# Scale and bias of the latents and of the first tile as columns behind their transposes, and a new order of the first transfers

## What is computed

```python
def layernorm(x, g, b, eps=1e-05):
    m = jnp.mean(x, axis=-1, keepdims=True)
    v = jnp.mean((x - m) ** 2, axis=-1, keepdims=True)
    return (x - m) / jnp.sqrt(v + eps) * g + b
...
xn = layernorm(x, ln_x_g, ln_x_b)
ln = layernorm(latents, ln_l_g, ln_l_b)
q = (ln @ Wq).reshape(b, m, h, d).transpose(0, 2, 1, 3)
kv = jnp.concatenate([xn @ Wkv, ln @ Wkv], axis=1)
...
qn = rmsnorm(q, qn_g) * scale
kn = rmsnorm(k, kn_g)
sim = jnp.einsum('bhid,bhjd->bhij', qn, kn)
```

## Time and profile before

| what | value |
|---|---|
| median of 3 runs | 240.18 us (240.14 to 240.39) |
| the profiled execution | 239.64 us |
| its span | 237.8 us |
| busy: PE, DVE, ACT, POOL | 225.6, 153.7, 150.0, 80.8 us |
| mean granted clock of TensorE | 0.993 |

### The profile page before, as it was taken

One profiled execution on the slowest core, in us unless ns is written; L12 is line 12 of the kernel. 1 busy time (PEld: TensorE's weight loads), 2 busy tenths in 40 slices (PEclk: granted clock), 3 DMA queues, 4 the chain that ended last, 5 costly groups with the idle time before them and its releaser, 6 DMA issues.

```text
span 237.8 us, 4203 instructions
## 1 busy us (share of the span) xinstructions
PE 225.6 (95%) x1475; PEld 194.6 (82%) x1475; DVE 153.7 (65%) x346; ACT 150.0 (63%) x329; POOL 80.8 (34%) x127
## 2 busy tenths in 40 slices
PE   7688999999989999999999999999999998999994
PEld 7354887786778989888898879899999987999883
DVE  1779999998688876867668655566665540312541
ACT  3355589889876769695766567777777655015141
POOL 5468776772464637473250500000000010100200
PEclk9799999999999999999999999999999999999999
DMA  5875101010000000000000799600000000000000
GB/s 181 301 216 206 48 22 44 25 31 16 1 21 3 0 6 0 0 0 3 0 3 0 240 428 328 160 0 3 0 4 0 0 4 0 0 3 0 0 3 22
DMA packets 11236, 13.80 MB, mean 58 GB/s; under 512 B 1584, under 2 KB 9936, under 8 KB 10960
## 3 DMA queue, kind: packets, MB, share of 16 engines
...
...
## 4 chain that ended last, share of the span: by engine, by line
PE 68%; DVE 15%; ACT 5%; POOL 4%; issue 4%; DMA 3%; SPq 1%; ACTq 0%; DVEq 0%; POOLq 0%
PE banks L1135 17%; PE banks L1010 13%; PE banks L1057 8%; PE banks L1086 8%; DVE small L778 5%; PE banks L1264 5%; PE banks L1156 4%; DVE sk L790 3%; DMA rows<-in_L_xattn_ln_x_b 3%; PE banks L1149 3%; PE banks L1088 2%; PE banks L1187 2%; PE banks L1289 1%; DVE raw L746 1%; POOL small L459 1%
## 5 line engine op out<-in xcount | busy, mean ns | idle before, releaser
L813 DVE TENSOR_TENSOR ptl<-banks,pth 128x512 fp32r<-128x512 f32 (+1 forms) x48 | 26.8, 558 | 28.6 <-ACT pth L576 27.6
L1135 PE MATMUL banks<-xnh,pth 128*128 128x256 f32 x128 | 37.6, 294 | 0.0
L1135 PE MATMUL banks<-xnh,ptl 128*128 128x256 f32 x128 | 36.3, 284 | 0.0
L1135 PE MATMUL banks<-xnl,pth 128*128 128x256 f32 x128 | 36.2, 283 | 0.0
L576 ACT ACTIVATE pth<-banks 128x512 fp32r<-128x512 f32 (+1 forms) x48 | 23.7, 493 | 11.3 <-PE banks L1010 10.2
L459 POOL TENSOR_TENSOR small<-small 128x16 f32<-128x16 f32 x7 | 20.4, 2908 | 29.2 <-DVE small L785 29.2
L523 ACT ACTIVATE sk<-banks 128x512 f32<-128x512 f32 x36 | 20.5, 606 | 13.4 <-PE banks L1057 13.3
L790 DVE TENSOR_TENSOR sk<-banks,small 128x512 f32<-128x512 f32 x36 | 23.0, 679 | 7.0 <-POOL small L459 6.9
L778 DVE TENSOR_REDUCE small<-sk 128x8 f32<-128x512 f32 x36 | 23.5, 678 | 4.0 <-ACT sk L523 3.9
L440 POOL COPY sp<-sp 128x64 f32<-128x64 f32 x16 | 4.1, 255 | 63.0 <-ACT sp L557 63.0
L1010 PE MATMUL banks<-ident,sp 128*128 128x128 f32 x144 | 24.4, 280 | 1.1 <-ACT sp L557 1.0
...
## 6 DMA issues: line engine op xcount, KB each, us to landing
knT<-in_L_attn_qkv_kernel SPq DMA_DIRECT2D x1, 3072.0 KB, 12.0
raw<-in_ctx SPq DMA_DIRECT2D x16, 128.0 KB, 2.1
knT<-in_L_xattn_Wq SPq DMA_DIRECT2D x1, 1024.0 KB, 9.2
wv<-in_L_xattn_Wkv SPq DMA_DIRECT2D x1, 1024.0 KB, 5.3
wout_sb<-in_L_xattn_Wout SPq DMA_DIRECT2D x1, 1024.0 KB, 5.5
knT<-in_L_attn_out_kernel SPq DMA_DIRECT2D x1, 1024.0 KB, 14.6
...
```

The lines of the kernel that those rows point to most:

```text
L813: nc.vector.tensor_tensor(ptl[:, j0:j1, :], banks[:, t3_bank(u, c), 0:(j1 - j0) * P].rearrange("p (j r) -> p j r", j=j1 - j0), pth[:, j0:j ...
L1135: nc.tensor.matmul(banks[:, u_bank(u), 0:D], p_[:, j, :], x_, start=(j == 0 and i == 0), stop=False)
```

## The change

In words, by engine:

- *Queues.* The four vectors ln_l_g, ln_l_b, ln_x_g and ln_x_b are also read as they lie, 2 rows of 128 each, into gb8 (8 x 128): two from SP's queue behind x, two from ScalarE's queue behind its weights. The rows of ln_l move behind tile 3 and the query weights, the rows of ln_x from behind tile 0 to behind tile 1, the query weights from behind tile 1 to behind tile 2. The latents' copies and the value weights move from behind tile 4 to behind tile 7. Tile 4 also waits for tile 0's transposes.
- *TensorE.* A transpose turns gb8 into 8 columns. The transposes of the latents and of tile 0 read the centred, scaled rows, without gain and bias. Item 0's second half takes its third product before the second. Keep_clock's 10 become 9 ahead of the latents and 4 behind.
- *ScalarE.* It copies the columns to gcols. For the latents and tile 0 it then applies gain and bias, which are now one number a partition, as it copies from the bank (scaled): twice each, once for xth and once in full fp32 (lnTf, x0Tf). L636's copy moves from item 3 to item 7.
- *VectorE.* The latents are centred and scaled in one operation in place of two. The low halves of the latents and of tile 0 are taken from the full copies. Statistics and centring of tiles 1 to 4 and sums of tile 5 stand at other places.
- *GpSimd.* The latents' rows lnf are made here, in item 1 (two operations of 128x256). The gains' product moves from item 0 to item 2, and tile 1's power ahead of tile 0's norm.

```diff
@@ -111,6 +111,9 @@
         gl = early(4, 0, D)
+        gb8 = early(2, 0, P)[0:8, :]
+        lmul = early(2, D, D)
+        x0Tf = early(2, 2 * D, D).rearrange("p (c r) -> p c r", c=DC)
         bl = early(4, D, D)
@@ -140,6 +143,7 @@
         mcol = small[:, 202:203]
+        gcols = small[:, 204:212]
@@ -338,6 +346,10 @@
+        def gain_rows(i, v):
+            return gb8[i * DC:(i + 1) * DC, :], v.rearrange("(c p) -> c p", p=P)
         def row(v):
@@ -350,19 +362,24 @@
             sp.dma_start(xb[:, :], x_rows).then_inc(w_x, 16)
-            sp.dma_start(gl, row(ln_l_g)).then_inc(w_lrows, 16)
-            sp.dma_start(bl, row(ln_l_b)).then_inc(w_lrows, 16)
+            for i, v in enumerate((ln_l_g, ln_l_b)):
+                sp.dma_start(*gain_rows(i, v)).then_inc(w_cols, 16)
             for k in range(B * NT):
...
                     sp.wait_ge(xn_ready, k - 3)
+                if k == 4:
+                    sp.wait_ge(xt_ps, 2)
                 sp.dma_start(raw[:, k % 4, :], ctx_tiles[k]).then_inc(w_ctx[k % 4], 16)
...
                     sp.dma_start(wraw[:, :, 512:1024], wkv_v[:, :, 512:1024]).then_inc(w_k[1], 16)
+                if k == 1:
                     sp.dma_start(rows[:, 0, :], row(ln_x_g)).then_inc(w_rows, 16)
                     sp.dma_start(rows[:, 1, :], row(ln_x_b)).then_inc(w_rows, 16)
-                if k == 1:
+                if k == 2:
                     sp.dma_start(wq_sb, wq_v).then_inc(w_q, 16)
                 if k == 3:
+                    sp.dma_start(gl, row(ln_l_g)).then_inc(w_lrows, 16)
+                    sp.dma_start(bl, row(ln_l_b)).then_inc(w_lrows, 16)
                     sp.dma_start(rows[:, 2, :], row(bout)).then_inc(w_bout, 16)
@@ -371,7 +388,7 @@
                                              g.rearrange("(d a) -> d a", a=1)).then_inc(w_gain, 16)
-                if k == 4:
+                if k == 7:
                     sp.wait_ge(ln_ready, 1)
@@ -424,6 +441,8 @@
                     pool.wait_ge(w_rows, 32)
+                if k == 1:
+                    pool.wait_ge(xn_ready, 1)
                 link(nc.gpsimd.tensor_tensor(xg[:, :], raw[:, k % 4, :], rows[:, 0, :], ALU.mult))
@@ -451,8 +470,8 @@
             nc.gpsimd.memset(mbias[:, :, J:KW], 0.0)
+            tile_rstd(1)
             tile_norm(0)
-            tile_rstd(1)
             for i in range(ITEMS):
@@ -465,7 +484,12 @@
                     context_low(i)
-                if i == 0:
+                if i == 1:
+                    pool.wait_ge(lat_hat, 1)
+                    pool.wait_ge(w_lrows, 32)
+                    link(nc.gpsimd.tensor_tensor(lmul, latg, gl, ALU.mult))
+                    nc.gpsimd.tensor_tensor(lnf, lmul, bl, ALU.add).then_inc(ln_ready, 1)
+                if i == 2:
@@ -498,6 +522,8 @@
             act.dma_start(wraw[:, :, 0:512], wkv_v[:, :, 0:512]).then_inc(w_k[0], 16)
+            for i, v in enumerate((ln_x_g, ln_x_b)):
+                act.dma_start(*gain_rows(2 + i, v)).then_inc(w_cols, 16)
@@ -505,6 +531,14 @@
                                      ACT.Copy).then_inc(xth_ready, 1)
+            def scaled(dst, n):
+                for c in range(DC):
+                    g = 2 * DC * n + c
+                    last = nc.scalar.activation(dst[:, c, :], banks[:, t1_bank(n), c * P:(c + 1) * P], ACT.Identity,
+                                                bias=gcols[:, g + DC:g + DC + 1], scale=gcols[:, g:g + 1])
+                return last
@@ -606,12 +640,17 @@
             wk_high(0)
-            xt_high(0)
-            nc.scalar.activation(lnTf, banks[:, t1_bank(0), 0:D].rearrange("p (c r) -> p c r", c=DC),
-                                 ACT.Copy).then_inc(lnT_ready, 1)
+            act.wait_ge(cols_ps, 1)
+            nc.scalar.activation(gcols, banks[:, 6, 0:4 * DC], ACT.Copy).then_inc(cols_ready, 1)
+            act.wait_ge(cols_ready, 1)
+            act.wait_ge(xt_ps, 1)
+            scaled(xth[:, 0], 0).then_inc(xth_ready, 1)
+            scaled(lnTf, 0).then_inc(lnT_ready, 1)
             wk_high(1)
             squares(0, 0)
-            xt_high(1)
+            act.wait_ge(xt_ps, 2)
+            scaled(xth[:, 1], 1).then_inc(xth_ready, 1)
+            scaled(x0Tf, 1).then_inc(x0T_ready, 1)
             squares(0, 1)
@@ -631,7 +670,7 @@
                     mask_bias(0, i == 9)
-                if i == 3:
+                if i == 7:
                     act.wait_ge(w_lat, 16 * 2 * B)
@@ -768,10 +807,15 @@
                 dve.wait_ge(xth_ready, n + 1)
+                full = banks[:, t1_bank(n), 0:D].rearrange("p (c r) -> p c r", c=DC)
                 if n == 0:
                     dve.wait_ge(lnT_ready, 1)
-                nc.vector.tensor_tensor(xtl[:, n % 2, :, :], banks[:, t1_bank(n), 0:D].rearrange("p (c r) -> p c r", c=DC),
-                                        xth[:, n % 2, :, :].bitcast(F32), ALU.subtract).then_inc(xtl_ready, 1)
+                    full = lnTf
+                if n == 1:
+                    dve.wait_ge(x0T_ready, 1)
+                    full = x0Tf
+                nc.vector.tensor_tensor(xtl[:, n % 2, :, :], full, xth[:, n % 2, :, :].bitcast(F32),
+                                        ALU.subtract).then_inc(xtl_ready, 1)
@@ -833,11 +877,8 @@
             dve.wait_ge(lat_mv, 1)
-            dve.wait_ge(w_lrows, 32)
-            nc.vector.scalar_tensor_tensor(latg, xb[:, :], lmv[:, 0:1], gl, ALU.subtract, ALU.mult).then_inc(lat_hat, 1)
-            dve.wait_ge(lat_hat, 1)
             dve.wait_ge(lat_rs, 1)
-            nc.vector.scalar_tensor_tensor(lnf, latg, lrs, bl, ALU.mult, ALU.add).then_inc(ln_ready, 1)
+            center(latg, xb[:, :], lmv[:, 0:1], lrs).then_inc(lat_hat, 1)
             tile_stats(0)
@@ -847,29 +888,29 @@
             wk_low(0)
+            xt_low(0)
             tile_center(0)
-            xt_low(0)
             wk_low(1)
+            key_norm2(0, 0)
             tile_stats(1)
-            key_norm2(0, 0)
             xt_low(1)
+            key_norm2(0, 1)
             tile_center(1)
-            key_norm2(0, 1)
             for i in range(ITEMS_A):
...
                     key_norm2(i, 1)
-                if i > 0:
+                if i > 1:
                     tile_mv(i + 3)
                 key_clamp(i)
-                if i == 0:
-                    tile_stats(2)
+                if i <= 1:
+                    tile_stats(i + 2)
                 else:
...
                 rn_at = own[0]
-                if i > 0:
+                if i > 1:
                     tile_sums(i + 4)
@@ -878,8 +919,10 @@
                     tile_center(2)
-                    tile_stats(3)
-                    tile_sums(4)
+                if i == 1:
+                    tile_stats(4)
+                    tile_center(3)
+                    tile_sums(5)
             key_norm2(ITEMS_A, 0)
@@ -1013,16 +1056,19 @@
                     pe.wait_ge(consts, 1)
-                    pe.wait_ge(ln_ready, 1)
-                    src = lnf
+                    pe.wait_ge(lat_hat, 1)
+                    src = latg
+                elif n == 1:
+                    pe.wait_ge(xhat_ready, 1)
+                    src = raw[:, 0, :]
                 else:
...
                 elif n >= 2:
                     pe.wait_ge(xtl_ready, n - 1)
-                    pe.wait_ge(lnT_ready, 1)
                 transposes(banks[:, t1_bank(n), :], lambda c: src[:, c * P:(c + 1) * P], DC).then_inc(xt_ps, 1)
@@ -1046,12 +1092,15 @@
                     pe.wait_ge(wk_hi, h + 1)
-                for k, (a, w) in enumerate(((xth, wkh), (xth, wkl), (xtl, wkh))):
-                    if k == 1 and i == 0:
+                order = ((xth, wkh), (xth, wkl), (xtl, wkh))
+                if i == 0 and h == 1:
+                    order = ((xth, wkh), (xtl, wkh), (xth, wkl))
+                for k, (a, w) in enumerate(order):
+                    if i == 0 and w is wkl:
                         if h == 1:
...
                         pe.wait_ge(wk_lo, h + 1)
-                    if k == 2:
+                    if a is xtl:
                         pe.wait_ge(xtl_ready, n + 1)
@@ -1156,8 +1205,11 @@
             pe.wait_ge(consts, 1)
-            keep_clock(10, 7)
+            keep_clock(9, 3)
+            pe.wait_ge(w_cols, 64)
+            nc.tensor.transpose(banks[:, 6, 0:4 * DC], gb8, ident[0:4 * DC, 0:4 * DC]).then_inc(cols_ps, 1)
             norm_transposed(0)
+            keep_clock(4, 3)
             for i in range(ITEMS_A + 1):
```

4 lines of the change are left out of this document (added).

## The result

Over 20 executions of each on one chip the changed kernel takes 241.37 us (239.87 to 242.52), the kernel before 240.31 (239.70 to 240.87): a ratio of 1.0031, 95% interval 1.0016 to 1.0047. It is slower by 0.3%, where 238.0 and faster was forecast. The profiled execution took 241.83 us, with a span of 240.0 and a mean granted clock of 0.993.

A forecast was written before the change was run, and what follows sets the result against it. VectorE's chain of square sums was taken as the bound, set by item 2's start. 3.4 - 1.05 + 0.28 - 0.45 = 2.2 us off 239.64 gives 237.4; 0.54 more for the median makes 238.0, range 236.8 to 239.3.

The forecast's parts named there:

- Columns and latents: Start of the kernel: columns land at 5.3, latents centred from 5.15, their transposes near 6.1, against 8.04.
- Rival A: Start: the columns land late, at 7.15, and the latents start 1.1 us later; gain 1.1, 239.1; chance 0.10.
- Second half of the weights: Start: with 256 KB less ahead of the transfer, ScalarE's second weights copy comes 1.0 to 1.3 us earlier, from 7.5.
- The four copies: ScalarE, latents and tile 0: four 128x128 copies at 0.277 us each, overlapping by 0.1, make about 0.85 us.
- Item 1: Item 1's square sums on VectorE start at 16.2, were 19.60: 3.4 us gained.
- Item 2: VectorE has about 4.7 us of work from item 1's start, as before; item 2 could start at 20.9 against 24.27.
- Item 3: GpSimd has tile 4's power only at 23.4, costing VectorE 1.05 us; item 3 at 25.7, was 28.00.
- L636's successor at item 7: ScalarE's latents' copy, moved to item 7, costs 0.45 us of its 0.62 there; leaving item 3 gives back 0.28.
- Rival C: TensorE's pause before tile 1's transposes lowers the clock: slower, 242.0, or 239.3 if brief; chance of slower 0.06.
- Rival B: Behind item 1 GpSimd sets the pace and two more 0.88 us hits eat the head start: gain 0.4, 239.8; chance 0.06.
- Rival D: The clock stays up through the start because TensorE's long pause is gone: gain 3.1, 237.1; chance 0.18.
- Rival E: New low halves of latents and tile 0 read two SBUF tensors, disturbing GpSimd: 0.8 less, gain 1.4, 238.8; chance 0.10.

## Why the prediction was wrong

The forecast's frame held: VectorE's chain sets the time, and item 3's start decides (3.0 us of delay at item 1 were 3.0 at the end of the stretch). The sum to that start did not: 25.7 was forecast, 28.53 came. By its steps, from the trace of the changed kernel:

- *Columns and latents*: right. Column transpose at 5.45, latents' at 5.64 (forecast 5.7 to 6.1), high half from 6.51. Rival A is out.
- *Second half of the weights*: forecast 7.5, came at 8.38 here, and between 7.4 and 8.4 in nine traces. That is 0.4 to 1.4 before the old 8.78. The old order's three traces have 6.2, 6.2 and 6.6 us from an issue at 2.56. I took the best end, and the 256 KB taken from in front of it did not buy 1.0 to 1.3 reliably. Where it lands at 7.5 little is won (next point): ScalarE is at its slower copies until 8.0 to 8.5, and the weights' copy starts at 7.90 to 8.40 in the nine.
- *The four copies*: mis-sized. 0.85 forecast, 1.5 measured. The 0.277 us was for a copy without columns; with them each next one starts some 0.35 after the last (11.03, then 11.72 two on) and takes 0.46 (0.81 for a pair, less 0.35). I had not looked up what the Trainium skill says here: "ScalarE: Activation LUTs", section "What ACT_TABLE_LOAD costs", adds about 93 ns for each operand that is a column. Two of them on the 0.277 are an estimate of 0.46, and the trace agrees. With the weights' copy late and the last transposed copies starting at 11.03 instead of 10.55, item 0's second sum starts at 13.05, not 12.15: **0.90**. Over the nine traces it lies between 12.49 and 13.23, so all of them miss.
- *Item 1*: 4.84 us from there, 4.05 forecast: **0.79**. The centrings take 0.95 and 0.81 beside GpSimd's operations instead of 0.42. The first ends 1.55 behind item 0's sum (14.60), 1.11 in the forecast, and passes these 0.44 on: from its end over GpSimd's norm and power to the second it is 2.56 (forecast 2.54), so VectorE's wait of 0.47 in front of the second is no loss of its own. The second and the step to the sum add 0.33. The row that shows 0.81 with such a wait was in my hands, and I priced at 0.42.
- *Item 2*: 5.16, forecast 4.7 "as much as before": **0.46**. VectorE doesn't wait once in this stretch. It has three statistics operations in it where the old kernel has one (two came a stage earlier), and no wait of 0.51 to hide them in.
- *Item 3*: 5.48, forecast 4.8 with its 1.05 for GpSimd's late power: **0.68**. The term's mechanism was right and its size wrong: 3.73 and the wait of 0.91, and then 0.41 more for the centring behind it (0.81) and 0.42 more for the clamp at 24.34 (0.59 instead of 0.17). What the step missed is first the collisions, and then that tile 3's centring, now behind the low half, is itself late, so that removing the two GpSimd operations alone gains little; the two runs apart and the one together show it.

The four add up to 2.83 us, which is 28.53 less 25.7. So at full clock nothing is left of the 2.2: item 3 starts at 28.07 in the trace with the filled pause, 0.07 after the old kernel's (that execution was 0.49 ahead already at item 0's second sum, 12.56).

- *L636's successor at item 7*: 0.45 forecast, 0.3 measured by moving it. The place costs more: items 7 and 8 stand 4.49 us apart against 3.82 in the old kernel, because the clamp there also takes 0.65 instead of 0.28 beside GpSimd's low part. At full clock the stretch from item 3 to item 10 takes 28.64, the old one 28.26: 0.38 given back, where 0.17 was forecast (0.45 less 0.28).
- *Rival C* has the sign and the mechanism, a pause on TensorE and the lower clock behind it, but I looked at one place only, in front of tile 1's transposes. There the pause was 1.03 us and the clock stayed up. It fell behind the pause of 2.35 us that my own term, GpSimd's late power, opens in front of item 2's key transposes: I let VectorE wait about a microsecond and never asked what TensorE does meanwhile. That is the step that turned "same" into "slower": it costs 1.2 us in 11 of 20 executions, and the run with six filling matmuls takes it away.
- *Rival B* (GpSimd's queue eats the head start) describes the full-clock kind, with more places than its two hits. I gave it 0.06; the main case took its durations from the favourable rows.
- *Rival D*: the clock does stay up at the start in the nine traces, and the sum shows nothing of 0.9 us from it. Its premise falls with the old kernel's own traces. The run with the old kernel's copy moved has the old start at a clock of 1.00 throughout, and item 1 comes 8.64 us after the broadcast row lands (11.39, 20.03); in the trace, with 1.2 GHz from about 9.3 to 12.7, it is 8.54 (11.06, 19.60). The low clock there cost nothing, since the row was what item 0's end waited for. Where it lasted to 16.3, in the run with two operations added, it is 9.19.
- *Rival E*: one hit is seen, GpSimd's xg at 12.74 with 0.91 beside the low half at 12.63, 0.17 more than the usual 0.73 to 0.74; and GpSimd's 128x1 operation at 6.48 took 1.25 beside the low weights. The rule cited there, of the Trainium skill's "GPSIMD Engine Reference", Specifications, agrees with these rows. But it names two kinds of VectorE instruction, two SBUF inputs and a two-port mode, and I weighed the first alone. The larger price was paid by the second kind: the Trainium skill's "VectorE: DVE Perf Modes", section "Mode 2×_2P — use both read ports for one tensor", has an operation with one source use both read ports when source and destination lie in SBUF, as the centring's do, and the centring is what goes from 0.4 to 0.8 and 0.95 beside GpSimd.

When a centring is slow can be read from the traces. In thirteen of them, up to 56 us, there are 166 centrings. The 50 that take 0.80 to 0.96 us are those where a GpSimd operation of 128x256 starts between 0.07 us before and 0.08 us after them. Where it starts 0.09 to 0.19 after them (14 times, as 22.53 behind 22.41), the centring keeps its 0.38 to 0.41 and GpSimd's operation takes 0.81 to 0.91 instead of 0.73; where it has been running for half a microsecond or more, both keep their times. From item 1 on, a centring that waited for its power always falls in the first group, because GpSimd's next operation, a low part, starts 0.07 ahead of it. So such a wait costs 0.4 us on top of its own length.

Left open: what sets where in 7.4 to 8.4 the weights land, and why the same pause lets the clock fall in one execution and not in the next.
